# Routed networks: the mask by a row of marks on VectorE instead of by a product on TensorE

## The reference

```
# layer 0: 8 experts, hidden width 128, the two best experts of each token
mask = one_hot(top_k(x @ Wg + bg, 2)).sum(-2)
h = gelu(einsum('td,edh->teh', x, W1) + b1)
y = einsum('teh,ehd->ted', h, W2) + b2
out = einsum('ted,te->td', y, mask)
# layer 3 (the last part): 8 experts, hidden width 256, the best expert, with a capacity
hmid = relu(x_of_expert @ w1 + b1);  y = hmid @ w2 + b2
y_tok = y * (prob * kept);  out = nan_to_num(y_tok, 0, posinf=1e4, neginf=-1e4)
```

## Time and profile before

| | |
|---|---|
| median of 3 runs | 3635.32 us (3634.79 to 3635.64) |
| the profiled execution | 3634.65 us, of which its span is 3632.9 us |
| TensorE, share of the span | 89% |
| DVE / ACT / POOL | 54% / 51% / 26% |
| mean granted clock of TensorE | 0.946 |
| layer 0's routed network | 686 to 836 us of the span |
| layer 3's routed network | 3324 to 3631 us of the span |
| matmuls of L419 | 576 records, 91 us of modelled duration, overlapping |

### The profile page before, as it was taken

The page is one execution under the profiler, slowest core; times in us unless marked ns, Lnnn a source line. Parts: engine busy times, 40 slices in busy tenths (PEclk is TensorE's granted clock), DMA queues, the critical chain, the costliest instruction groups (busy, mean ns, idle before and its releaser), DMA issues. The chain is left out here.

```text
span 3632.9 us, 65471 instructions
## 1 busy us (share of the span) xinstructions
PE 3243.0 (89%) x24843; PEld 2090.2 (58%) x24843; DVE 1961.1 (54%) x3986; ACT 1837.2 (51%) x4211; POOL 941.3 (26%) x938
## 2 busy tenths in 40 slices
PE   6999988798989898878988959997699999986999
PEld 6999976444655555436755633334466666663444
DVE  4666645204444445335947744445699999944111
ACT  2333334456465655555643523335466666643665
POOL 0000001000000000103726612223477777720000
PEclk9999999899999999988989969998799999987999
DMA  2000000000000000000000012220000000000000
GB/s 71 14 14 14 12 17 6 6 1 7 3 4 3 4 3 4 4 3 7 2 8 1 1 46 62 56 52 15 18 4 5 5 5 5 3 19 3 7 9 9
DMA packets 41518, 48.36 MB, mean 13 GB/s; under 512 B 9158, under 2 KB 38696, under 8 KB 40744
## 3 DMA queue, kind: packets, MB, share of 16 engines
q1 hardware_dynamic: 41208, 44.19, 4.6%
HBM read 38.47 MB, written 2.38 MB: 11 GB/s over the span
## 5 line engine op out<-in xcount | busy, mean ns | idle before, releaser
L463 ACT ACTIVATE p_hidden<-p_hid_ps,net_bias 128x344 f32<-128x344 f32 x816 | 383.8, 548 | 251.4 <-PE p_hid_ps L419 175.3
L436 PE MATMUL p_y_ps<-p_hidden,net_down 128*64 128x344 f32 x1632 | 281.7, 468 | 0.0
L413 PE MATMUL p_hid_ps<-xn,net_up 64*128 64x344 f32 x1248 | 253.5, 487 | 16.0 <-PEq L2225 13.1
L2121 POOL TENSOR_TENSOR p_qt<-p_qt,p_q_sum 97x512 f32<-97x512 f32 (+1 forms) x44 | 46.3, 1053 | 769.2 <-DVE p_q_sum L2075 769.2
L2424 DVE TENSOR_TENSOR p_hid<-p_silu,p_pair_ps 128x344 f32<-128x344 f32 x288 | 134.8, 509 | 173.3 <-PE p_pair_ps L2373 93.8
L2405 ACT ACTIVATE p_silu<-p_pair_ps 128x344 f32<-128x344 f32 x288 | 116.0, 454 | 200.6 <-PE p_pair_ps L2362 200.6
L1604 POOL TENSOR_TENSOR p_rot<-p_rot,p_cross 128x512 f32<-128x512 f32 x128 | 159.8, 1271 | 177.1 <-DVE p_cross L1741 177.1
L2598 PE MATMUL p_c_ps<-p_in,p_c1w 128*128 128x126 f32 (+5 forms) x960 | 173.0, 311 | 32.0 <-POOL p_in L2671 32.0
L1617 POOL TENSOR_TENSOR p_prob<-p_prob,p_total 128x1024 f32<-128x1024 f32 (+1 forms) x128 | 185.4, 1470 | 15.9 <-DVE p_total L1767 15.9
L436 PEld LDWEIGHTS p_y_ps<-p_hidden,net_down 128*64 128x64 f32 x1632 | 100.2, 137 | 151.9 <-ACT p_hidden L463 52.4
L154 PE MATMUL p_var_ps<-p_square,average 128*128 128x344 f32 x432 | 171.2, 484 | 11.4 <-ACT p_square L170 11.4
(11 more groups left out here) (428 smaller groups left out, 8026.8 us busy)
## 6 DMA issues: line engine op xcount, KB each, us to landing
p_row<-gated_rows SPq DMA_DIRECT2D x192, 86.0 KB, 2.8
p_x<-in_tok_x SPq DMA_DIRECT2D x32, 192.0 KB, 2.3
out<-h SPq DMA_DIRECT2D x12, 172.0 KB, 1.8
p_swapped<-xn SPq DMA_DIRECT2D x64, 32.0 KB, 1.9
p_c3w<-in_tok_c3w SPq DMA_DIRECT2D x1, 1280.0 KB, 9.4
thirds_fold<-in_L_fold SPq DMA_DIRECT2D x1, 1156.5 KB, 5.1
gated_w<-in_L2m_w SPq DMA_DIRECT2D x2, 512.0 KB, 4.3
p_val_high<-shared_values SPq DMA_DIRECT2D x1, 1024.0 KB, 6.8
```

The costliest lines, as they stand in the source:

```text
L413: mm = pe.matmul(hid_ps[k % ring][:, 0:TILE], w_up[half(g), n, :], x[half(g), cols(t)], start=True, stop=not experts)
L436: mm = pe.matmul(y_ps[u][half(g), 0:TILE], w_down[:, n, :], hid[k % hidden_ring][:], start=n == 0, stop=last and not experts)
L463: act.activation(hid[k % hidden_ring][:], hid_ps[k % ring][:, 0:TILE], func, bias=b_up[:, n:n + 1]).then_inc(act_done.sem, 1)
```

## The change

The products of L419 go. `gate_phase` makes `marks16`, a bf16 copy of the marks, instead of `unmarked`. At the start of the phase SP stores the 8 rows of marks of each half to DRAM (two transfers) and waits for both; then, for each tile and expert, it loads that row twice (one transfer for each half), repeated over all 128 partitions, into one of 6 buffers `row`. DVE multiplies each `hid` buffer in place by its row once ACT has written it, and the lowering waits for that (`masked`) instead of for ACT. The endings of a tile move behind steps of the next tile in DVE's order: in layer 3 `weigh` behind the masks of block 4, `compare` behind block 6, the rest behind block 9; in layer 0 the addition behind block 4. The stores of tiles are put between the loads of rows in SP's order.

```
+            outside = nc.dram_tensor(f"mark_rows{tower.phases}", [HALVES, EXPERTS, COLS], BF16, kind="Internal").ap()
...
                         mm = pe.matmul(hid_ps[k % ring][:, 0:TILE], w_up[half(g), n, :], x[half(g), cols(t)],
-                                       start=True, stop=not experts)
-                        if not experts:
-                            mm.then_inc(up_done.sem, 1)
-                    for g in range(HALVES if experts else 0):
-                        k = HALVES * s + g
-                        pe.matmul(hid_ps[k % ring][:, 0:TILE], tower.banish[half(g), experts.of(n), :],
-                                  experts.unmarked[half(g), cols(t)], start=False,
-                                  stop=True).then_inc(up_done.sem, 1)
+                                       start=True, stop=True)
+                        mm.then_inc(up_done.sem, 1)
...
-                        pe.wait_ge(act_done.sem, act_done.at(k + 1))
+                        if experts:
+                            pe.wait_ge(masked.sem, masked.at(k + 1))
+                        else:
+                            pe.wait_ge(act_done.sem, act_done.at(k + 1))
...
+                if experts:
+                    for g in range(HALVES):
+                        sp.dma_start(outside[g, :, :], experts.marks16[D * g:D * g + EXPERTS, :]).then_inc(
+                            put_out.sem, 16)
+                    sp.wait_ge(put_out.sem, put_out.at(32))
+                for x in range(uses):
+                    t, e = x // EXPERTS, x % EXPERTS
+                    if x >= row_ring:
+                        sp.wait_ge(masked.sem, masked.at(HALVES * experts.parts * (x - row_ring + 1)))
+                    for g in range(HALVES):
+                        sp.dma_start(row[x % row_ring][:, g, :], outside[g, e:e + 1, cols(t)].to_broadcast(
+                            [P, TILE])).then_inc(landed[x % row_ring].sem, 16)
+                    if store is not None and e == EXPERTS - 1 and t >= 1:
+                        sp.wait_ge(y_read.sem, y_read.at(t))
+                        sp.dma_start(store[:, cols(t - 1)], finish.acc[:, cols(t - 1)]).then_inc(stored.sem, 16)
...
+                def mask(s):
+                    x = s // experts.parts
+                    for g in range(HALVES):
+                        k = HALVES * s + g
+                        dve.wait_ge(act_done.sem, act_done.at(k + 1))
+                        if g == 0:
+                            dve.wait_ge(landed[x % row_ring].sem, landed[x % row_ring].at(32 * (x // row_ring + 1)))
+                        dve.tensor_tensor(hid[k % hidden_ring][:], hid[k % hidden_ring][:], row[x % row_ring][:, g, :],
+                                          ALU.mult).then_inc(masked.sem, 1)
...
+                for t in range(TILES):
+                    for n in range(blocks if experts else 0):
+                        mask(blocks * t + n)
+                        if n == 4 and t >= 1 and in_parts:
+                            weigh(t - 1)
+                        if n == 6 and t >= 1 and in_parts:
+                            finish.compare(dve, t - 1)
+                        if n == (9 if in_parts else 4) and t >= 1:
+                            add(t - 1)
```

More of the change, by code:

```diff
@@ L229, in gate_weights, with gate_phase @@
         ("w", [P, HALVES * EXPERTS], f"{layer}_gate_w"), ("b", [CHUNK, HALVES * EXPERTS], f"{layer}_gate_b")])
-def gate_phase(tower, x, gate, top, weighted, rows_t, unmarked=None):
+def gate_phase(tower, x, gate, top, weighted, rows_t, marks16=None):
     nc = tower.nc
@@ L363, in _ @@
                 v.total = done[0]
-                for n, (c0, k) in enumerate(groups if unmarked is not None else []):
+                for n, (c0, k) in enumerate(groups if marks16 is not None else []):
                     at = slice(c0 * CHUNK, (c0 + k) * CHUNK)
                     dve.wait_ge(copied.sem, copied.at(n + 1))
-                    dve.tensor_scalar(unmarked[:, at], rows_t[:, at], -1.0, None, ALU.add)
+                    dve.tensor_copy(marks16[:, at], rows_t[:, at])
         if not (top == 1 or weighted):
@@ L374, in mlp_phase @@
     nc, ring, span = tower.nc, 4, 2
-    hidden_ring = 8
+    hidden_ring, row_ring = 8, 6
     with phase(tower) as ph:
@@ L392, in mlp_phase @@
             load(ph)
+        uses = TILES * EXPERTS if experts else 0
+        if experts:
+            row = [ph.sb(f"row{r}", [P, HALVES, TILE], BF16) for r in range(row_ring)]
+            landed = [ph.counts(32 * len(range(r, uses, row_ring))) for r in range(row_ring)]
+            put_out, masked = ph.counts(32), ph.counts(HALVES * steps)
+            outside = nc.dram_tensor(f"mark_rows{tower.phases}", [HALVES, EXPERTS, COLS], BF16, kind="Internal").ap()
         aux_sb = [ph.sb(f"aux_sb{u}", [P, TILE]) for u in range(2)] if finish.broadcast else None
@@ L481, in _ @@
             def _(sp):
-                for t in range(TILES if store is not None else 0):
+                if experts:
+                    for g in range(HALVES):
[12 more added lines that the diff above has]
+                        sp.dma_start(store[:, cols(t - 1)], finish.acc[:, cols(t - 1)]).then_inc(stored.sem, 16)
+                for t in range(TILES - 1 if store is not None else TILES, TILES):
                     sp.wait_ge(y_read.sem, y_read.at(t + 1))
@@ L489, in _, with wait_output @@
             def _(dve):
-                for t in range(TILES):
-                    u = t % 2
+                def mask(s):
[7 more added lines that the diff above has]
+                                          ALU.mult).then_inc(masked.sem, 1)
+                def wait_output(t):
                     if experts:
@@ L497, in _, with weigh, add @@
                         dve.wait_ge(aux_ready.sem, aux_ready.at(t + 1))
-                    finish.vector(dve, y_ps[u][:, 0:TILE], aux_sb and aux_sb[u], cols(t), t).then_inc(
-                        y_read.sem, 1)
+                def weigh(t):
+                    wait_output(t)
+                    finish.weigh(dve, y_ps[t % 2][:, 0:TILE], aux_sb[t % 2], t)
+                def add(t):
+                    if not in_parts:
+                        wait_output(t)
+                    finish.vector(dve, y_ps[t % 2][:, 0:TILE], aux_sb and aux_sb[t % 2], cols(t), t).then_inc(
+                        y_read.sem, 1)
+                in_parts = experts and finish.broadcast is not None
+                for t in range(TILES):
[7 more added lines that the diff above has]
+                            add(t - 1)
+                    if not experts:
+                        add(t)
+                if in_parts:
+                    weigh(TILES - 1)
+                    finish.compare(dve, TILES - 1)
+                if experts:
+                    add(TILES - 1)
         if not experts:
@@ L504, with __init__ @@
 class Experts:
[L507 to L511, removed]
+    def __init__(self, marks, marks16, parts):
+        self.marks, self.marks16, self.parts = marks, marks16, parts
 class AddTo:
@@ L2178, in broadcast, with weigh, compare @@
                          start=True, stop=True)
-    def vector(self, dve, y, aux, cols, t):
+    def weigh(self, dve, y, aux, t):
         u, step = t % 2, t + 1
-        tmp = self.tmp[u]
-        dve.scalar_tensor_tensor(tmp[:], y, self.bias, aux[:], ALU.add,
-                                 ALU.mult).then_inc(self.made.sem, 1)
+        dve.scalar_tensor_tensor(self.tmp[u][:], y, self.bias, aux[:], ALU.add, ALU.mult).then_inc(self.made.sem, 1)
         dve.wait_ge(self.made.sem, self.made.at(step))
-        if not self.finite:
-            return dve.tensor_tensor(self.acc[:, cols], self.acc[:, cols], tmp[:], ALU.add)
-        ends = self.ends[u]
+    def compare(self, dve, t):
+        u, step = t % 2, t + 1
+        tmp, ends = self.tmp[u], self.ends[u]
         dve.tensor_scalar(ends[:, 0, :], tmp[:], LARGEST, 10000.0, ALU.is_gt, ALU.mult)
@@ L2197, in vector @@
         dve.wait_ge(self.compared.sem, self.compared.at(step))
+    def vector(self, dve, y, aux, cols, t):
+        u, step = t % 2, t + 1
+        tmp = self.tmp[u]
+        if not self.finite:
+            self.weigh(dve, y, aux, t)
+            return dve.tensor_tensor(self.acc[:, cols], self.acc[:, cols], tmp[:], ALU.add)
+        ends = self.ends[u]
         dve.tensor_tensor(ends[:, 0, :], ends[:, 0, :], ends[:, 1, :], ALU.add).then_inc(self.joined.sem, 1)
@@ L2511, in capacity_ffn @@
         rows_t = stack.enter_context(nc.sbuf_tensor("cap_rows", [P, COLS], F32))
-        unmarked = stack.enter_context(nc.sbuf_tensor("cap_unmarked", [P, COLS], BF16))
+        marks16 = stack.enter_context(nc.sbuf_tensor("cap_marks16", [P, COLS], BF16))
         net, gate = network(stack, tower, ("L3", ""), "L3_down_b"), gate_weights(stack, tower, "L3")
@@ L2515, in capacity_ffn @@
         norm_phase(tower, h, x, 1e-5, loads=net.loads + gate.loads + pick.loads)
```

(10 more changed lines are left out.)

## The result

The changed kernel takes 3720.88 us (median of 4, 3718.5 to 3728.5) against 3635.06 before: 1.0241 times as long, 95% interval 1.0223 to 1.0259. It is 2.4% slower; 3608 was forecast. The profiled execution took 3728.5 us with a span of 3726.7.

The account below looks back on a forecast made before the run. TensorE was taken to bound both routed networks: -41.8 us for mask products, +0.6 for the last masks at the networks' ends, +9.4 for late starts and +5.0 for the clock give -26.8, so 3608 us, range 3599 to 3628.

Parts of the forecast that it names:

- TensorE's 2.67 us a pair: In both routed networks, a pair of steps without mask products takes 2.67 us instead of 2.96; -41.8 us over 144 pairs.
- The masks on DVE: Four multiplications a pair at 0.47 us each, 1.9 us of 2.67, cost nothing on the path in steady state.
- The endings: Tile endings split into parts between DVE's masks: 0 to 0.5 us a tile, 0 to 6 in all, taken as 0.
- The start: First lowering 9.6 us after each network's phase starts: +9.4 us together, plus +5.0 us for a slower clock.
- The clock: Half clock behind the pause at each network's start: 2.5 us a network, bounds 0 and 3.0, +5.0 us together.
- SP's issues: Two load issues for each expert and tile take 0.9 to 1.28 us, inside layer 0's step of 1.33 but barely.
- issues that grow with the packets: Were SP's issue to grow with the packets (two times 1.28 us), layer 0 would take 96 x 1.23 = 118 us more.
- The transfers: Loads of mask rows: 18 packets an engine at 50 ns, 0.9 us a use, hidden within layer 0's 1.33 us.
- the three rows: Packet prices read from the trace: 25 ns for ordinary 512-byte loads, 77 and 99 ns for L2341's packets, all from one row.
- a packet costs the same at half its size, because all engines read one row of DRAM: Rival: 99 ns a packet, 1.78 us a use, layer 0 takes 43 us more, 3651 us in total; chance 0.10.
- the sum: All terms together, -26.8 us: layer 0 gains 13.9 and pays 7.3, layer 3 gains 27.8 and pays 7.7.

Follow-up runs that it names:

- padded version: The changed kernel with rows of marks 9344 bytes apart in DRAM instead of 8256; 3601.73 us.
- interleaved: The changed kernel with both halves' rows side by side in DRAM, one transfer of 1376-byte packets replacing two of 688; 3601.68 us, 0.9913 of before.
- ring_3: The changed kernel with 3 buffers for rows instead of 6; 3724.28 us.
- whole_endings: The interleaved kernel with layer 3's ending of a tile in one go behind the masks of block 4; 3620.5 us, 0.9963 of before.
- early_rows: The interleaved kernel with layer 3's rows stored and its first six loaded during the phase before; 3595.4 us, 0.9893 of before.
- early_padded: The early_rows kernel with 17664 bytes from expert to expert instead of 16512; 3596.76 us, 0.9896 of before.
- pitch_12352: The changed kernel with 12352 bytes from row to row in DRAM instead of 8256; 3603.03 us.

## Why the prediction was wrong, step by step

- *TensorE's 2.67 us a pair.* Right: 2.66 in layer 3, and 2.66 in layer 0 of the padded version.
- *The masks on DVE.* Right: 4 in 1.83 us, hidden in layer 3 and, where rows are there, in layer 0. The bf16 operand shows no effect (504 to 521 ns, as the 0.52 us for two f32). A mask cost 0.46 us in a row of four, for 0.47.
- *The endings.* Right, and the order matters: with the endings in one piece layer 3 takes 22.7 us more (18.8 in the medians).
- *The start.* The delay was taken too long. First lowerings came 8.6 and 7.3 us after the first raising, not 9.6, so 6.2 us of delay and not 9.4. The clock was about right: 2.5 a network was forecast, and in layer 3 it took 2.7 in the interleaved kernel, behind a wait of 4.15 us, and 1.65 in the changed one, behind 3.03.
- *SP's issues.* Right: 0.43 us in the median in the padded version, two of them inside 1.33. The changed kernel's 1.22 in layer 0 looks like the prediction's case of issues that grow with the packets, "96 x 1.23 = 118 us", and the size is near the loss of 116.4, but by luck: ring_3 keeps the pace with issues of 0.42.
- *The transfers.* This is the step that failed: "For packets half as long I take 50 ns, between the first two, 0.9 us a use: hidden". A packet took 107 ns, above the dearest of the three rows, and a use took 2.69 us. The price was taken to go by size, between a row with own lines and one with a shared line; it goes by whether lines are shared and where they lie. The shared lines of `gated_rows`, at 77 and 99 ns, have a pitch of 16512 bytes, 128 off 16 KB, so they were the nearest row, and the value of 50 leaned away from it. A second error makes the price weigh more but did not decide: a use was counted as 18 packets on engines that are full. 18 x 107 is 1.93, but the engines are busy 72 to 74%, and 1.93 / 0.73 = 2.6. At 50 to 58 ns the loads stayed hidden all the same. Why the engines stand idle for a quarter of the time while rows are late stays open: the views give the mean of the 16 alone.
- The rival "a packet costs the same at half its size, because all engines read one row of DRAM" named the place, the sign and half of the mechanism, with a chance of 0.10 and 3651 us; it missed the idle engines and that the pitch decides.

With padding alone the kernel takes 3601.7 us with its networks 7.3 and 20.6 us shorter than before; the sum forecast 6.6 and 20.1. So the other terms held as a sum, to within a microsecond a network.

The Trainium skill's page "DMA: Bandwidth & Descriptors", section "Latency and other measured facts", tells of copies that fall to half their rate at row pitches of large powers of two, that 4 KB of padding cures and 192 bytes don't, and gives channels of the memory as an inference. Here 64 bytes beside 8192 don't help and 1152 do (107 and 55 ns), at pitches far smaller than that page's, and only for lines that many read: 128 own lines 16384 bytes apart took 40 ns.

## What to carry to other kernels

A row spread over partitions by repeated reads of DRAM is not an ordinary load: take its price from a row of the trace that repeats a line at a like pitch, and compare the bytes per second that the new loop needs with those reached in long stretches. Lay such rows out at a pitch well off a multiple of 8 KB, or put what is read together side by side, before anything else is changed. And where a product leaves the bounding engine for a chain through another engine, ask when its first input is there: moving layer 3's first loads one phase ahead was worth 6.9 us of its network.

## What the runs showed of the hardware

- Packets that repeat one line of DRAM, in layer 0: of 688 bytes 107 ns where the lines lie 8256 or 16384 bytes apart, and 50 to 58 ns at pitches of 9344, 12288 and 12352; of 1376 bytes 110 to 121 ns at 16512 (whole_endings, early_rows, interleaved) and 67 at 17664 (early_padded). From own lines, 38 and 40 ns at 8256 and 16384.
- 16 copies spread over the partitions of a transfer (8 readers a copy) bring it to 36 ns as well, but the first load could be issued only 42 us after the first of the 32 stores of 8 rows of 8256 bytes, 1.3 us a store.
- A share of 73% of the engines was the queue's limit in the changed kernel: rows landed 9.6 us after their issue, and with half as many under way 6.1 us, at the same pace. The same share is no sign of it by itself: at 75.0% (pitch_12352) and 77.2% (interleaved) the rows came nearly all in time.
